# Layer 0 of a two-way scan stack: the gate product written into the sigmoid's SBUF buffer instead of its PSUM bank

## The chip, the cores and the metric

The kernel runs on one core of a Trainium2 chip. The time is in microseconds of the device for one launch of the whole kernel; lower is better. Its engines work at the same time, each through its own queue of instructions in a fixed order: TensorE (PE in the profile) multiplies matrices and writes to PSUM, VectorE (DVE), ScalarE (ACT) and GpSimd (POOL) compute on SBUF and PSUM, and SyncE (SP) issues the transfers. An engine stops at an instruction that waits for a semaphore, and everything behind it in its queue stops too.

## What is computed

Eight batches of 512 tokens with 512 features. A stack of four layers runs over the tokens, once forwards and once backwards, with the same weights for both directions; a fusion product and a feed-forward part follow.

```python
def _mingru(x, Wz, bz, Wh, bh):
    z = jax.nn.sigmoid(jnp.einsum('bsi,hi->bsh', x, Wz) + bz)
    h_tilde = jnp.tanh(jnp.einsum('bsi,hi->bsh', x, Wh) + bh)
    a = jnp.clip(1.0 - z, CLAMP_LO, CLAMP_HI)
    return _linear_scan(a, z * h_tilde)      # h[t] = a[t] * h[t-1] + z[t] * h_tilde[t]
...
    for i in range(L):                        # L = 4
        h_new = _mingru(h, Wz[i], bz[i], Wh[i], bh[i])
        if i > 0:
            h_new = h_new + h
        h = _layernorm(h_new, gamma, beta)
...
h_fwd = _stack(x, ctx_1024, cond_1024, ctx_1024, cond_1024, ...)
h_bwd = _stack(jnp.flip(x, axis=1), ctx_1024, cond_1024, ctx_1024, cond_1024, ...)
x = x + fusion(concatenate([h_fwd, flip(h_bwd)]))
x = x + ffn(layernorm(x))
```

Wz and Wh are the same matrix, and so are the biases, so one matrix product serves sigmoid and tanh. In layer 0 both directions have the same input: the product and its gates are computed once, and two scans, one over the tokens forwards and one backwards, read them.

## The kernel before

The features lie on the 128 partitions in four blocks m = 0 to 3, the 512 tokens along the free axis. A **job** is (batch, direction, layer); the 56 jobs stand in the list `JOBS` in an order written out by hand, and a layer-0 job serves both directions, so there are eight of them, at places 0, 1, 12, 17, 26, 31, 40 and 45 of the list. Each job has four gate products, numbered i = 4k + m through the whole program. They go through these steps:

- `mm` (TensorE, L498): twelve matmuls of 128x512 into the PSUM bank `GATE[i % 3]`, one of three banks that the gates take in turn. Before it overwrites the bank it waits until the scan of product i - 3 is done (`s_sc`).
- `gates` (ScalarE, L794 and L795): the sigmoid of minus the product, which is 1 - z, goes to the SBUF buffer `yb[i % 3]`, and the tanh goes back into the PSUM bank.
- `keep` (GpSimd, L1519): the clipped copy `ab[i % 3]` of `yb`, which is the reference's a.
- `blend` (VectorE, L1070): (1 - yb) times the tanh, written over the tanh in the PSUM bank.
- `scan` (VectorE): from layer 1 on, one scan (L1082) of `ab` and the bank, written over `yb`, and GpSimd adds the layer's input (`add`, L1528). In layer 0 there are two scans: L1090 forwards into `H[s]`, L1091 backwards into `H[s + 1]`.

After that a job's output is normalized over the features: `tokens` (TensorE, L518) turns it with 128x128 transposes into five PSUM banks used as a ring, `stats` (VectorE, L1102 and L1105) takes mean and variance into `mvp`, `inv` (GpSimd, L1537 to L1547) makes scale and shift by four small instructions on 128x2 values (`vep`, `nmp`, `rsp`, `nbp`), `norm` (ScalarE, L806) writes `ntok`, `back` (TensorE, L532) turns it back, `feature` (ScalarE, L831 and L835) and `low` (VectorE, L1114) split it into a high part `AH` and a rest `AL`, from which the next layer's products are made.

What sets the order is the queue of each engine, written out in slots: one slot per job, in which every engine does a fixed mixture of steps of that job and of its neighbours. In VectorE's slot the job's four scans stand among the `low` and `stats` steps of other jobs. GpSimd has, beside `keep`, `add` and `inv`, the preparation of weights: rests of the layer weights at the start (`low_weights`, L1560 and L1562), and from the middle on the pieces of the later weights (`excess`, L1601 and L1603, and `rest`, L1611). After the last job comes the second part of the kernel (fusion, L552; feed-forward, L583 and L602), which the change leaves alone; its instructions L1221, L1281 and L1295 on VectorE and L1648 on GpSimd are quoted below.

Of the kernel before, what the change touches and what calls it, by code (L numbers as in the profile page):

```python
# [7 lines left out]
ALU = mybir.AluOpType  # L8
# [21 lines left out]
def behind(j):  # L30
# [12 lines left out]
JOBS = [  # L43
# [23 lines left out]
def place(t):  # L67

    return 2 * (t[0] % 2) + t[1]
# [144 lines left out]
def pixart_block(nc, x, wt, cond, fwt, fb, gamma, beta, fct, lnw, lnb, pjt, out):  # L214
# [8 lines left out]
    def sb(stack, name, shape, dt=F32):  # L223
        return stack.enter_context(nc.sbuf_tensor(name, shape, dt))

    def sem(name):
        return ctx.enter_context(nc.semaphore(name))
# [50 lines left out]
    for s in (0, 1, 3, 2):  # L278
        AH[s] = sb(p1, f"AH{s}", [128, KC, S], F32R)
        AL[s] = sb(p1, f"AL{s}", [128, KC, S], F32R)  # L280
    H = [sb(p1, f"H{s}", [128, KC, S]) for s in range(4)]
# [3 lines left out]
    yb = [sb(p1, f"yb{i}", [128, S]) for i in range(3)]  # L285
    ab = [sb(p1, f"ab{i}", [128, S]) for i in range(3)]
# [54 lines left out]
    GATE = PS[0:3]  # L341
# [29 lines left out]
    s_wd, s_nc, s_cn, s_a, s_sf, s_sc, s_bs, s_ag, s_ve, s_nm = (  # L371
        sem(n) for n in ("s_wd", "s_nc", "s_cn", "s_a", "s_sf", "s_sc", "s_bs", "s_ag", "s_ve", "s_nm"))
# [8 lines left out]
    s_c, s_wp, s_p, s_v, s_rs, s_nb, s_xr, s_xb, s_pp, s_pl = (  # L381
        sem(n) for n in ("s_c", "s_wp", "s_p", "s_v", "s_rs", "s_nb", "s_xr", "s_xb", "s_pp", "s_pl"))
# [25 lines left out]
    def stored(t):  # L408

        return 16 * (t[0] // 2 + 1)  # L410

    @block.tensor
    def _(e):
# [62 lines left out]
        def mm(k, m):  # L476

            if k is None:
                return
            b, d, l = JOBS[k]  # L480
            s, i = place(JOBS[k]), 4 * k + m
            if i >= 3:
                e.wait_ge(s_sc, i - 2)
            n = 0
            for q in range(KC):
                if m == 0:
                    e.wait_ge(s_al, LOWS[("x", b, q) if l == 0 else ("h", TAIL[(b, d, l - 1)], q)])
                    if k == JOB[(0, 0, l)]:
                        if l == 0:
                            e.wait_ge(s_w0, q + 1)  # L490
                        else:
                            e.wait_ge(s_wh, 4 * l - 3 + q)
                        if (l, q) in WEIGHT_P:
                            e.wait_ge(s_wp, WEIGHT_P.index((l, q)) + 1)
                        else:
                            e.wait_ge(s_wd, WEIGHT_D.index((l, q)) + 1)
                for w, a in ((WH[l], AH[s]), (WL[l], AH[s]), (WH[l], AL[s])):
                    r = e.matmul(GATE[i % 3][:], w[:, q, m * 128:(m + 1) * 128], a[:, q, :], start=(n == 0), stop=(n == 11))  # L498
                    n += 1
            r.then_inc(s_mm, 1)  # L500
# [142 lines left out]
        back("x", 0, 0)  # L643
        fold_row(1)
        mm(0, 0)
        mm(0, 1)
        back("x", 1, 0)
        back("x", 1, 2)
        mm(0, 2)
        back("x", 1, 3)  # L650
        back("x", 1, 1)
# [96 lines left out]
        for j in range(NB * NC):  # L748
            b, c = j // NC, j % NC
# [313 lines left out]
    def _(e):  # L1063
        def blend(k, m):
            if k is None:
                return
            i = 4 * k + m
            c = i % 3
            e.wait_ge(s_t, i + 1)
            e.scalar_tensor_tensor(GATE[c][:], yb[c][:], 1.0, GATE[c][:], ALU.subtract, ALU.mult, reverse0=True).then_inc(s_p, 1)  # L1070

        def scan(k, m):
            if k is None:
                return
            b, d, l = JOBS[k]
            i = 4 * k + m
            c = i % 3
            e.wait_ge(s_a, i + 1)
            e.wait_ge(s_p, i + 1)
            if l > 0:  # L1080
                rv = slice(None, None, -1) if d else slice(None)
                e.tensor_tensor_scan(yb[c][:, rv], ab[c][:, rv], GATE[c][:, rv], 0.0, ALU.mult, ALU.add).then_inc(s_sc, 1)  # L1082
                return
            s = 2 * (b % 2)
            if b >= 2 and m == 0:
                e.wait_ge(d_hs[s], stored((b - 2, 0, 3)))
                e.wait_ge(d_hs[s + 1], stored((b - 2, 1, 3)))

                e.wait_ge(s_t1, max(T1N[("T", TAIL[(b - 2, i, 3)], p, 1)] for i in (0, 1) for p in (0, 1)) + 1)
            e.tensor_tensor_scan(H[s][:, m, :], ab[c][:], GATE[c][:], 0.0, ALU.mult, ALU.add).then_inc(s_sf, 1)  # L1090
            e.tensor_tensor_scan(H[s + 1][:, m, :][:, ::-1], ab[c][:, ::-1], GATE[c][:, ::-1], 0.0, ALU.mult,  # L1091
                                 ALU.add).then_inc(s_sc, 1)

        def stats(tau, pr):
# [252 lines left out]
        low("x", 0, 3)  # L1347
        low_weights(1, 0)
        blend(0, 0)
        scan(0, 0)  # L1350
        blend(0, 1)
        low("x", 1, 0)
        scan(0, 1)
        blend(0, 2)
        low("x", 1, 1)
        low("x", 1, 2)
        scan(0, 2)
        blend(0, 3)
        low("x", 1, 3)
# [111 lines left out]
        for j in range(NB * NC):  # L1471
            b, c = j // NC, j % NC
# [510 lines left out]
```

## Time and profile before

| | us |
|---|---|
| median of 3 runs | 1561.7 (1561.46 to 1562.28) |
| the profiled execution's own time | 1561.99 |
| its span in the profile | 1559.8 |
| TensorE busy | 1526.0 (98%) |
| VectorE busy | 1343.0 (86%) |
| ScalarE busy | 1027.5 (66%) |
| GpSimd busy | 1033.5 (66%) |

The profile is of one execution. Busy time is the sum of the time in which an engine has an instruction under way; matmuls overlap, so a group's mean duration (408 ns for a 128x512 matmul) is longer than the distance at which they follow each other. The granted clock of TensorE is 1.0 of its full speed, so it runs at the higher of its two levels, 2.4 GHz, throughout. The layers take the first 890 us, in which VectorE is busy to nine tenths and more in most slices.

### The profile page before, as it was taken

The numbers are of one execution on the slowest core, as the hardware profiler recorded it, in microseconds if no ns is written. First come the engines' busy times: TensorE is split into PE (matmuls) and PEld (weight loads), VectorE is DVE, ScalarE is ACT, GpSimd is POOL, SyncE is SP. The second block draws the span as 40 slices with busy tenths as digits, with TensorE's granted clock in tenths as the row PEclk, the third lists the DMA queues.
The fourth block names the chain that finished last, engine by engine and source line by source line (L and its number), as shares of the span: only waits on it lengthen the run. The fifth ranks groups of instructions, "written<-read, shape, count | busy, mean of one in ns | idle before, by whom it ended". The sixth has DMA issues, their size and how long they took to land.

```text
span 1559.8 us, 22974 instructions
## 1 busy us (share of the span) xinstructions
PE 1526.0 (98%) x7690; PEld 1256.8 (81%) x7690; DVE 1343.0 (86%) x1919; ACT 1027.5 (66%) x1689; POOL 1033.5 (66%) x1267
## 2 busy tenths in 40 slices
PE   6999999999999999999999999999999999999999
PEld 4777888788878788888888878888888888888887
DVE  7997989989999989899888878798888878787876
ACT  6888979889687898687897544544444444444454
POOL 4766766767868678777688745465556556565566
PEclk9999999999999999999999999999999999999999
DMA  4111121413312111212124462020202021111101
GB/s 169 38 65 55 70 101 34 162 41 108 109 41 84 39 55 68 95 55 83 67 82 163 156 217 61 1 88 21 89 21 88 21 69 40 62 48 32 36 14 41
DMA packets 72865, 112.66 MB, mean 72 GB/s; under 512 B 5159, under 2 KB 37927, under 8 KB 69678
## 3 DMA queue, kind: packets, MB, share of 16 engines
q1 hardware_dynamic: 72750, 111.21, 21.1%
q8 instruction: 62, 1.02, 0.3%
q14 instruction: 53, 0.43, 0.1%
HBM read 73.43 MB, written 37.76 MB: 71 GB/s over the span
## 4 chain that ended last, share of the span: by engine, by line
PE 70%; DVE 5%; ACT 4%; issue 1%; POOL 1%; POOLq 0%; ACTq 0%; DVEq 0%
PE ps L498 21%; PE ps L583 15%; PE ps L602 15%; PE ps L552 11%; PE ps L518 3%; PE ps L532 3%; DVE bnp L1102 1%; ACT H L831 1%; ACT AH L835 1%; PE ps L565 1%; DVE H L1091 1%; DVE H L1090 1%; DVE AL L1114 1%; ACT ps L795 1%; ACT yb L794 1%
## 5 line engine op out<-in xcount | busy, mean ns | idle before, releaser
L498 PE MATMUL ps<-AH,WH 128*128 128x512 f32 x896 | 366.0, 408 | 8.9 <-DVE H L1091 6.8
L498 PE MATMUL ps<-AL,WH 128*128 128x512 f32 x896 | 350.6, 391 | 0.0
L498 PE MATMUL ps<-AH,WL 128*128 128x512 f32 x896 | 349.7, 390 | 0.0
L1648 POOL TENSOR_TENSOR acq<-acq,sq 128x512 f32<-128x512 f32 x120 | 181.8, 1515 | 151.6 <-ACT sq L926 151.1
L1528 POOL TENSOR_TENSOR H<-H,yb 128x512 f32<-128x512 f32 x192 | 250.6, 1306 | 34.6 <-DVE yb L1082 28.2
L1082 DVE TENSOR_TENSOR_SCAN yb<-ab,ps 128x512 f32<-128x512 f32 x192 | 232.4, 1211 | 10.7 <-POOL ab L1519 3.1
L913 ACT ACTIVATE g<-ps 128x512 f32<-128x512 f32 x128 | 76.4, 597 | 249.6 <-PE ps L583 249.6
L794 ACT ACTIVATE yb<-ps,ncnd 128x512 f32<-128x512 f32 x224 | 157.7, 704 | 121.7 <-PE ps L498 118.6
L1519 POOL TENSOR_SCALAR ab<-yb 128x512 f32<-128x512 f32 x224 | 139.0, 621 | 118.5 <-ACT yb L794 106.4
L1281 DVE SCALAR_TENSOR_TENSOR gl<-g,wcol,gh 128x512 fp32r<-128x512 f32 x118 | 133.9, 1135 | 93.3 <-ACT gh L923 93.3
L498 PEld LDWEIGHTS ps<-AH,WH 128*128 128x128 f32 x896 | 168.6, 188 | 46.0 <-DVE H L1091 9.3
L498 PEld LDWEIGHTS ps<-AL,WH 128*128 128x128 f32 x896 | 168.2, 188 | 36.4
L498 PEld LDWEIGHTS ps<-AH,WL 128*128 128x128 f32 x896 | 169.0, 189 | 29.0
L1102 DVE BATCH_NORM_STATS2 bnp<-ps 128x6 f32<-128x512 f32 x256 | 165.2, 685 | 30.6 <-PE ps L518 29.7
L1295 DVE TENSOR_TENSOR acc<-acc,g 128x512 f32<-128x512 f32 x120 | 189.2, 1577 | 0.0
L1070 DVE SCALAR_TENSOR_TENSOR ps<-yb,ps 128x512 f32<-128x512 f32 x224 | 152.3, 680 | 21.7 <-ACT ps L795 20.9
L1114 DVE TENSOR_TENSOR AL<-ps,AH 128x512 fp32r<-128x512 f32 x224 | 147.0, 674 | 19.9 <-ACT AH L835 19.1
L831 ACT ACTIVATE H<-ps,bet,gam 128x512 f32<-128x512 f32 x192 | 155.1, 808 | 3.1 <-PE ps L532 2.9
L806 ACT ACTIVATE ntok<-ps,nbp,rsp 128x512 f32<-128x512 f32 x192 | 139.3, 782 | 16.4 <-POOL nbp L1547 15.8
L835 ACT ACTIVATE AH<-ps 128x512 fp32r<-128x512 f32 x224 | 139.6, 628 | 3.3 <-PE ps L532 3.3
L518 PE MATMUL ps<-ident,H 128*128 128x128 f32 x1024 | 132.6, 273 | 7.4 <-ACT ntok L806 6.4
L518 PEld LDWEIGHTS ps<-ident,H 128*128 128x128 f32 x1024 | 117.5, 140 | 24.7 <-ACT ntok L806 8.6
(172 smaller groups left out, 3308.6 us busy)
## 6 DMA issues: line engine op xcount, KB each, us to landing
hs_scratch<-H SPq DMA_DIRECT2D x16, 1024.0 KB, 5.6
hc<-hs_scratch SPq DMA_DIRECT2D x32, 512.0 KB, 4.4
xr<-in_x SPq DMA_DIRECT2D x32, 256.0 KB, 4.5
out<-ob SPq DMA_DIRECT2D x32, 256.0 KB, 2.2
xbuf<-in_x SPq DMA_DIRECT2D x7, 1024.0 KB, 7.9
RAW<-in_wt SPq DMA_DIRECT2D x16, 256.0 KB, 6.6
stg<-in_fct SPq DMA_DIRECT2D x16, 256.0 KB, 3.1
stg<-in_pjt SPq DMA_DIRECT2D x16, 256.0 KB, 3.2
```

The costliest lines, as they stand in the source:

```text
L498: r = e.matmul(GATE[i % 3][:], w[:, q, m * 128:(m + 1) * 128], a[:, q, :], start=(n == 0), stop=(n == 11))
L518: r = e.transpose(RING[n % 5][:, m * 128:(m + 1) * 128], H[s][:, m, c:c + 128], ident[:])
L552: r = e.matmul(FUSED[u, h][:], a[u % 2][:, q, :], w[:, q, :], start=(n == 0), stop=(n == 11))
L583: r = e.matmul(HIDDEN[j % 2][:], FC[q][:, c * 128:(c + 1) * 128], a[b % 2][:, q, :], start=(n == 0), stop=(n == 7))
L602: r = e.matmul(PROJ[t][:], a[BUFFER[j]][:, t * 128:(t + 1) * 128], PJ[c], start=(c == 0 and a is gh), stop=(c == NC - 1 and a is gl))
L794: e.activation(yb[c][:], GATE[c][:], ACT.Sigmoid, bias=ncnd[:, l, m:m + 1], scale=-1.0).then_inc(s_y, 1)
L831: e.activation(H[s][:, m, :], RING[n][:], ACT.Identity, bias=bet[:, m:m + 1], scale=gam[:, m:m + 1]).then_inc(s_h, 1)
L1082: e.tensor_tensor_scan(yb[c][:, rv], ab[c][:, rv], GATE[c][:, rv], 0.0, ALU.mult, ALU.add).then_inc(s_sc, 1)
L1102: e.bn_stats(bnp[:, r, i, :], RING[BANK[u] % 5][:]).then_inc(s_bs, 1)
L1295: e.tensor_tensor(acc[b % 2][:], acc[b % 2][:], g[j % 2][:], ALU.add).then_inc(f_s1, 1)
L1528: e.tensor_tensor(H[s][:, m, :], H[s][:, m, :], yb[i % 3][:], ALU.add).then_inc(s_v, 1)
L1648: e.tensor_tensor(acq[b % 2][:], acq[b % 2][:], sq[:], ALU.add).then_inc(f_s2, 1)
```

## The change

In layer 0 the blend writes its product into `yb[i % 3]`, over the sigmoid, and both scans read it there, so that the PSUM bank is free after the blend. The product i of `mm` therefore waits for the blend of i - 3 (`s_p`) where i - 3 is of layer 0, and for its scan as before in the other layers. Since the blend now overwrites what `keep` reads, it waits for GpSimd's `keep` of the same product (`s_a`), for which before only the scan waited. The sigmoid of product i still waits for the scans of i - 3 before it writes `yb`.

```diff
@@ mm
-            if i >= 3:
+            if i >= 3 and JOBS[(i - 3) // 4][2] == 0:
+                e.wait_ge(s_p, i - 2)
+            elif i >= 3:
                 e.wait_ge(s_sc, i - 2)
@@ blend
             e.wait_ge(s_t, i + 1)
-            e.scalar_tensor_tensor(GATE[c][:], yb[c][:], 1.0, GATE[c][:], ALU.subtract, ALU.mult, reverse0=True).then_inc(s_p, 1)
+            if JOBS[k][2] == 0:
+                e.wait_ge(s_a, i + 1)
+            dst = yb[c] if JOBS[k][2] == 0 else GATE[c]
+            e.scalar_tensor_tensor(dst[:], yb[c][:], 1.0, GATE[c][:], ALU.subtract, ALU.mult, reverse0=True).then_inc(s_p, 1)
@@ scan
-            e.tensor_tensor_scan(H[s][:, m, :], ab[c][:], GATE[c][:], 0.0, ALU.mult, ALU.add).then_inc(s_sf, 1)
-            e.tensor_tensor_scan(H[s + 1][:, m, :][:, ::-1], ab[c][:, ::-1], GATE[c][:, ::-1], 0.0, ALU.mult,
+            e.tensor_tensor_scan(H[s][:, m, :], ab[c][:], yb[c][:], 0.0, ALU.mult, ALU.add).then_inc(s_sf, 1)
+            e.tensor_tensor_scan(H[s + 1][:, m, :][:, ::-1], ab[c][:, ::-1], yb[c][:, ::-1], 0.0, ALU.mult,
                                  ALU.add).then_inc(s_sc, 1)
```

No instruction is added, removed or moved on any engine: 32 blends write elsewhere, 64 scans read their second input elsewhere, and the waits of the products behind 32 of them and of the 32 blends differ.

## Rows read from the trace of the kernel before

**Rows 1.** the page: the span line and the engines' busy times.

```profile
span 1559.8 us, 22974 instructions
...
PE 1526.0 (98%) x7690; PEld 1256.8 (81%) x7690; DVE 1343.0 (86%) x1919; ACT 1027.5 (66%) x1689; POOL 1033.5 (66%) x1267
```

**Rows 2.** whom TensorE waited for: us in total, times, longest.

```profile
PE ps L498 <- DVE H L1091: 6.8, 6, 1.9
PE ps L518 <- ACT ntok L806: 6.4, 9, 0.7
```

**Rows 3.** three lines' instructions: duration in ns min/median/max, first and last start.

```profile
L1091 DVE TENSOR_TENSOR_SCAN H<-ab,ps x32: 1191/1194/1197, 25.6 to 742.3; 128x512 f32<-128x512 f32 x32
...
L1295 DVE TENSOR_TENSOR acc<-acc,g x120: 677/1779/1791, 922.5 to 1546.6; 128x512 f32<-128x512 f32 x120
...
L1537 POOL TENSOR_SCALAR vep<-mvp x128: 191/191/1663, 39.1 to 917.1; 128x2 f32<-128x2 f32 x128
```

**Rows 4.** timeline of VectorE, then GpSimd: start us, length us, line.

```profile
1013.17 1.78 DVE L1295 TENSOR_TENSOR acc<-acc,g 128x512 f32<-128x512 f32 x1
...
917.55 1.20 DVE L1221 TENSOR_TENSOR hcl<-hc,hch 128x1024 fp32r<-128x1024 f32 x1
...
1013.06 1.33 POOL L1648 TENSOR_TENSOR acq<-acq,sq 128x512 f32<-128x512 f32 x1 [5.50 <-ACT sq L926]
...
917.15 1.66 POOL L1537 TENSOR_SCALAR vep<-mvp 128x2 f32<-128x2 f32 x1 [1.71 <-DVE mvp L1105]
```

**Rows 5.** timeline of VectorE, batch 4's layer-0 job.

```profile
435.49 0.68 DVE L1070 SCALAR_TENSOR_TENSOR ps<-yb,ps 128x512 f32<-128x512 f32 x1
436.36 1.22 DVE L1090 TENSOR_TENSOR_SCAN H<-ab,ps 128x512 f32<-128x512 f32 x1 [0.19 <-POOL ab L1519]
...
438.61 0.67 DVE L1070 SCALAR_TENSOR_TENSOR ps<-yb,ps 128x512 f32<-128x512 f32 x1
...
439.99 1.21 DVE L1090 TENSOR_TENSOR_SCAN H<-ab,ps 128x512 f32<-128x512 f32 x1
...
447.20 0.30 DVE L1105 BATCH_NORM_AGGREGATE mvp<-bnp 128x2 f32<-128x6 f32 x2
```

**Rows 6.** timeline of GpSimd over the same stretch.

```profile
435.71 0.62 POOL L1519 TENSOR_SCALAR ab<-yb 128x512 f32<-128x512 f32 x1
436.41 1.28 POOL L1528 TENSOR_TENSOR H<-H,yb 128x512 f32<-128x512 f32 x1
437.77 0.61 POOL L1519 TENSOR_SCALAR ab<-yb 128x512 f32<-128x512 f32 x1
438.48 0.77 POOL L1601 TENSOR_SCALAR stg<-raw,th,nth 128x512 f32<-128x512 f32 x1
439.33 1.29 POOL L1603 TENSOR_TENSOR stg<-raw,stg 128x512 f32<-128x512 f32 x1
...
448.85 0.19 POOL L1547 TENSOR_TENSOR nbp<-nmp,rsp 128x2 f32<-128x2 f32 x1
```

**Rows 7.** timeline of ScalarE and TensorE there; idle time and releaser in brackets.

```profile
450.01 1.45 ACT L806 ACTIVATE ntok<-ps,nbp,rsp 128x512 f32<-128x512 f32 x2
...
449.78 0.50 PE L498 MATMUL ps<-AH,WH 128*128 128x512 f32 x1 [0.97 <-DVE H L1091]
...
452.64 1.91 PE L532 MATMUL ps<-ident,ntok 128*128 128x128 f32 x16
```

**Rows 8.** timeline at the start: VectorE, GpSimd, TensorE.

```profile
24.47 1.22 DVE L1090 TENSOR_TENSOR_SCAN H<-ab,ps 128x512 f32<-128x512 f32 x1
...
26.71 0.67 DVE L1070 SCALAR_TENSOR_TENSOR ps<-yb,ps 128x512 f32<-128x512 f32 x1
...
23.89 1.57 POOL L1560 TENSOR_SCALAR RAW<-RAW,gam 128x512 f32<-128x512 f32 x1
25.54 1.30 POOL L1562 TENSOR_TENSOR WL<-RAW,WH 128x512 fp32r<-128x512 f32 x1
...
35.47 0.50 PE L498 MATMUL ps<-AH,WH 128*128 128x512 f32 x1 [1.12 <-DVE AL L1114]
```

## The prediction

> **What bounds the kernel now.** I read the page first, to see which engine could set the end: TensorE is busy for 1526.0 of a span of 1559.8 us, VectorE for 1343.0 [rows 1]. All that TensorE does not do costs time, and at most some 34 us can be won. The second view is the table of waits, to see what TensorE's gaps come from [rows 2]. Six times a product waited for a layer-0 backward scan (L1091), 6.8 us in sum: once for each of the six layer-0 jobs after the start, and this is what the edit to `mm` removes. Nine times a transpose of `tokens` waited for ScalarE's `norm`, 6.4 us in sum, with nothing over 0.7 us; that chain comes from VectorE's `stats` through GpSimd's `inv`. So TensorE is held up a little, by a VectorE that is behind for a moment after a layer-0 job. The third view is the timeline around such a job, to see whether VectorE has room there [rows 5 to 7]; in it VectorE has almost no idle time, so a delay on it is handed on.
>
> **The wait that goes.** In batch 4 the product at 449.78 sat idle for 0.97 us for the scan [rows 7]. The blend of that product, third of the job, had ended more than 3 us before that, so by the new rule TensorE would go on at once. The gain is bounded by nothing and by the 6.8 us of the table. I don't expect to keep it even if nothing else changed: the next waits of TensorE, for ScalarE's `norm` [rows 2], hang on VectorE's queue, which this wait does not speed up, so they grow by most of what is won here.
>
> **The wait that comes.** The blend must now wait for `keep`. For block 0 of batch 4 the blend began at 435.49, while `keep` began at 435.71 and took 0.62 [rows 5, 6]: it would start at 436.35, 0.86 later. The forward scan had stood 0.19 idle for the same `keep` and began at 436.36; behind a blend of 0.68 it now begins at 437.1, 0.7 later. For the other blocks `keep` is done before the blend (437.77 plus 0.61 against 438.61) as long as GpSimd is not late. Queued behind the waiting blend on VectorE are the scans, the `low` and `stats` steps of other jobs, and TensorE and ScalarE wait for those.
>
> **The scans' second input, the largest term.** A scan now reads two SBUF tensors, which none in this trace does. What the trace shows is how the two classes of VectorE instruction behave beside GpSimd. With one input in PSUM, the 32 backward scans take 1191 to 1197 ns whatever GpSimd is doing [rows 3], and the scan at 436.36 ran its 1.22 us under a GpSimd add begun at 436.41 [rows 5, 6]. With two inputs in SBUF, the additions of L1295 take 677 ns at best, but 1779 in the median and 1791 at most [rows 3]: the one at 1013.17 took 1.78 us, and GpSimd's two-input add had begun at 1013.06 for 1.33 us; VectorE stood until it had ended [rows 4]. It goes the other way too: GpSimd's small `vep` takes 191 ns, but 1663 at most [rows 3], and that one, at 917.15, ended at 918.81, with the two-input subtraction of VectorE that ran from 917.55 to 918.75 [rows 4]. So the two exclude each other for whole instructions, and take turns. The price of a scan in SBUF is thus bounded by nothing, as for the scans now, and by the remainder of a GpSimd instruction each, up to 1.3 us; I take the second, because the rows nearest to it in what they read (two SBUF tensors, same size) have it.
>
> The Trainium skill says the same for the class: on its page "SBUF — State Buffer", under "Who interferes with whom", a VectorE instruction with two SBUF inputs contends with a GpSimd instruction that reads SBUF, and one with at most one SBUF input does not. That is a rule that speaks against this change; rows 3 and 4 agree with it for additions and subtractions, and no run here shows a scan of this kind.
>
> **Batch 4 worked out.** Two scans take 2.25 us on VectorE (436.36 to 438.61), 1.12 each [rows 5]. Forward scan of block 0: ready at 437.1, held by the add begun at 436.41 (1.28 us) until 437.6, done at 438.7. `keep` of block 1, which was to start at 437.77, gets its turn next, to 439.3 [rows 6]. Backward scan: 439.3 to 440.4. The blend of block 1 starts at 440.4 where it was 438.61: VectorE is 1.8 late. GpSimd resumes at 440.4 with L1601 (0.77) and L1603 (1.29) [rows 6], to 442.5; the forward scan of block 1, at 439.99 before, is ready at 441.8 and held for 0.6; a `keep` slips in before the backward one, 0.5. VectorE is 2.9 late when it comes to the aggregate of 447.20, which starts `inv` [rows 5]. Right behind it stand the scans of block 2 and 3, and the four small instructions of `inv` fall between them: the first waits for a forward scan (1.1), the second for the backward one (1.1), the last for the next forward scan (0.9 of it), so `inv` takes 3.0 longer. `nbp`, before from 448.85 to 449.04 [rows 6], ends 5.9 later. ScalarE's two norms started at 450.01, 0.97 after it, and took 1.45, to 451.46; TensorE's transposes started at 452.64, 1.18 after that [rows 7]. That is all the cover there is: 2.15. TensorE is 5.9 - 2.15 = 3.8 late there. If the small instructions are not held, it is 2.9 - 2.15 = 0.8 at this place, but some 3 at the next `norm` for which TensorE already waits today, as VectorE is itself about 3.2 late by the end of the four scan pairs and has no idle time in which to catch up before. I take 3.2 for a job, with 1.8 and 3.8 as the bounds. The absent wait of 0.97 is in this, as all is reckoned against the starts of before.
>
> Batches 4 to 7 have this pattern: 4 x 3.2 = 12.8. Batches 2 and 3 come before L1601 and L1603 begin, and keep only the 1.8 of block 0 and the 3.0 of `inv`, less the same cover of 2.15: 2.65 each, which I round to 2.6, so 5.2.
>
> **The start.** Beside the first products GpSimd prepares weights with L1560 (1.57 us) and L1562 (1.30), one after the other [rows 8]. The scan at 24.47 would be held until 25.46, 1.0, and its backward partner by L1562, 1.2: 2.2 for the product. The pair stands beside the second product too, 2.2. The third has its blend behind a late `keep`, 0.7. In sum 5.1 on a VectorE that goes from 24.47 to the end of the fourth product's `low` without a pause, and there TensorE already waits 1.12 us for it, at 35.47 [rows 8], so all 5.1 reach TensorE. Batch 1 meets the same two instructions twice more, but TensorE has work of its own there; between 0 and 4, I take 1.0.
>
> **The sum.** 5.1 + 1.0 + 5.2 + 12.8 = 24.1 us. On the profiled execution's 1561.99 that is 1586.1, and as the median lay 0.3 lower, **1585.8 us**, 1.5% slower. Nothing after the last job changes.
>
> **The rivals.**
> 1. *The scans don't exclude GpSimd.* A scan takes 1.12 us for 512 columns, nearly twice an addition, and may read so slowly that both are served. Then the new `keep` wait remains, about 1.2 at the start, where GpSimd's `keep` stands behind the long preparations, and 0.7 of VectorE in five jobs, which eats the removed stall at the next `norm`: between 0 and +2 in all, 1562.5. For it: no scan in the trace reads two SBUF tensors. Against it: all other two-input instructions are held.
> 2. *Faster: the freed bank carries through.* The same, but `norm` comes earlier too, since ScalarE's queue starts earlier when the product does. All of L1091's 6.8 us would be kept [rows 2]: 1561.7 - 6.8 = 1554.9. It decides if ScalarE's lateness and not VectorE's aggregate sets `norm`. Against it: a saturated VectorE, and the `keep` wait.
> 3. *Excluded, but small instructions are not*, and part of the delay falls into gaps: 1.8 for four jobs, 1.0 for two, 3 at the start, so 12: 1574. I count it in the forecast's own range.
>
> That the change doesn't do what it says is possible only in part: where VectorE is late, the blend is late too, and a product may wait for it in place of the scan. This is inside the first case.
>
> **How the numbers follow.** The exclusion, with its range of 1571 (rival 3 and a little less) to 1597 (3.8 for four jobs, 2.6 for two, 9 at the start, and some 5 for delays that feed one another), has 0.76; rival 1 has 0.17, rival 2 0.07. A tenth of the first case lies outside its range. To leave out no more than 2 in 10 the whole range must reach down to rival 1: 1561 to 1597. A measurement of this kernel can tell 0.2%, 3 us, from no change. Slower by more than that: 0.76 and 0.03 of rival 1, 0.79; within: 0.13, nearly all of rival 1 with a little of rival 2; faster: 0.08, rival 2 and a tail of rival 1.
>
> **What the new profile would show.** If right: the scans of layer 0 no longer take some 1.2 us each but reach 2 us and more, GpSimd's `vep`, `nmp` or `nbp` show durations over 1 us around 232 to 745 us, the blend has idle time put down to GpSimd's `ab`, no product waits for L1091's successor, and TensorE's waits for `norm` or for `low` at the start are longer by some 20 us in sum. If the scans keep their 1.2 us, the largest term is wrong and rival 1 or 2 holds. If they are held but TensorE's waits grow by less than 10 us, it is the cover that I have misjudged.

## The result, and the profile after

| | before, us | changed, us |
|---|---|---|
| median | 1561.85 (1561.46 to 1562.28, 4 runs) | 1586.11 (1585.08 to 1587.89, 4 runs) |
| ratio | | 1.0154 (95% interval 1.0141 to 1.0167) |
| span of the profiled execution | 1559.8 | 1584.6 |
| GpSimd busy | 1033.5 | 1073.5 |

The change costs 24.3 us, 1.5%. The page of the changed kernel, its lines that answer to [rows 1], and the costliest new idle time:

```profile
span 1584.6 us, 23006 instructions
...
PE 1534.8 (97%) x7690; PEld 1260.9 (80%) x7690; DVE 1354.9 (86%) x1919; ACT 1028.8 (65%) x1689; POOL 1073.5 (68%) x1267
...
L534 PE MATMUL ps<-ident,ntok 128*128 128x128 f32 x896 | 118.2, 281 | 29.7 <-ACT ntok L808 16.7
```

The page counts 32 instructions more: the blends' waits for `s_a`, the same 32 as in the run with the blend's wait alone (23006) and absent where only the scans' input is changed (22974). TensorE and VectorE are hardly busier (8.8 and 11.9 us more), GpSimd by 40 us, though its compute instructions are the same 1267: time in which an instruction of it is held counts as busy. The line of `back` (L534, before L532) now has 29.7 us of idle time before it. The table of waits of TensorE, which answers to [rows 2] (us in sum, times, longest):

```profile
PE ps L534 <- ACT ntok L808: 16.7, 10, 2.6
...
PE ps L500 <- DVE AL L1119: 7.4, 7, 2.4
PE ps L520 <- ACT ntok L808: 6.9, 9, 1.2
```

The six waits for L1091 are gone, as the diff says. In their place stand ten waits of `back` for ScalarE's `norm`, 16.7 us (0.7 before), and seven of products for VectorE's `low` (7.4, before 1.1 in one).

**The held instructions.** Durations of the layer-0 scans and of three of the small instructions of `inv`, in ns min/median/max, which answer to [rows 3]:

```profile
L1095 DVE TENSOR_TENSOR_SCAN H<-ab,yb x32: 1201/1225/1929, 23.8 to 765.8; 128x512 f32<-128x512 f32 x32
...
L1096 DVE TENSOR_TENSOR_SCAN H<-ab,yb x32: 1192/1200/2256, 25.0 to 767.0; 128x512 f32<-128x512 f32 x32
...
L1542 POOL TENSOR_SCALAR vep<-mvp x128: 192/193/1664, 42.4 to 941.9; 128x2 f32<-128x2 f32 x128
...
L1544 POOL TENSOR_SCALAR nmp<-mvp x96: 192/193/1103, 42.6 to 885.8; 128x2 f32<-128x2 f32 x96
...
L1552 POOL TENSOR_TENSOR nbp<-nmp,rsp x96: 195/197/1098, 43.7 to 886.8; 128x2 f32<-128x2 f32 x96
```

The backward scans took at most 1197 ns before; now the slowest takes 2256. The small instructions that take 0.19 us alone show up to 1.1 us (`vep` had its one of 1.66 already before). Most scans are still at 1.2: only those that met a reading GpSimd are longer. (In this kernel no instruction of GpSimd has a PSUM bank as an operand; all read and write SBUF.)

**Batch 4's job.** VectorE and GpSimd in the timeline of the changed kernel, which answer to [rows 5, 6]. TensorE's work was 12.05 us later than before when the job began, so a start at 448.53 stands against 435.49 + 12.05 = 447.54.

```profile
448.53 0.69 DVE L1075 SCALAR_TENSOR_TENSOR yb<-yb,ps 128x512 f32<-128x512 f32 x1 [0.91 <-POOL ab L1524]
449.31 1.56 DVE L1095 TENSOR_TENSOR_SCAN H<-ab,yb 128x512 f32<-128x512 f32 x1
450.79 1.56 DVE L1096 TENSOR_TENSOR_SCAN H<-ab,yb 128x512 f32<-128x512 f32 x1
452.28 0.66 DVE L1075 SCALAR_TENSOR_TENSOR yb<-yb,ps 128x512 f32<-128x512 f32 x1
...
453.46 1.93 DVE L1095 TENSOR_TENSOR_SCAN H<-ab,yb 128x512 f32<-128x512 f32 x1
455.31 1.19 DVE L1096 TENSOR_TENSOR_SCAN H<-ab,yb 128x512 f32<-128x512 f32 x1
...
461.39 0.30 DVE L1110 BATCH_NORM_AGGREGATE mvp<-bnp 128x2 f32<-128x6 f32 x2
461.61 1.20 DVE L1095 TENSOR_TENSOR_SCAN H<-ab,yb 128x512 f32<-128x512 f32 x1
462.73 1.20 DVE L1096 TENSOR_TENSOR_SCAN H<-ab,yb 128x512 f32<-128x512 f32 x1
```

```profile
447.81 0.61 POOL L1524 TENSOR_SCALAR ab<-yb 128x512 f32<-128x512 f32 x1
448.51 1.28 POOL L1533 TENSOR_TENSOR H<-H,yb 128x512 f32<-128x512 f32 x1
449.88 1.40 POOL L1524 TENSOR_SCALAR ab<-yb 128x512 f32<-128x512 f32 x1
451.38 1.55 POOL L1606 TENSOR_SCALAR stg<-raw,th,nth 128x512 f32<-128x512 f32 x1
453.02 1.28 POOL L1608 TENSOR_TENSOR stg<-raw,stg 128x512 f32<-128x512 f32 x1
...
461.77 1.02 POOL L1542 TENSOR_SCALAR vep<-mvp 128x2 f32<-128x2 f32 x1 [0.42 <-DVE mvp L1110]
462.88 1.04 POOL L1544 TENSOR_SCALAR nmp<-mvp 128x2 f32<-128x2 f32 x1
463.88 0.71 POOL L1549 TENSOR_TENSOR rsp<-vep,nhalf 128x2 f32<-128x2 f32 x1
464.73 1.09 POOL L1552 TENSOR_TENSOR nbp<-nmp,rsp 128x2 f32<-128x2 f32 x1
```

The blend waits 0.91 us for `keep`. The forward scan of block 0 is held by the add begun at 448.51, which has 0.48 us to go, and takes 1.56. Then `keep` of block 1, which was issued at 449.88, gets its turn and the backward scan waits for it, 1.56. L1606 in turn waits for that scan (1.55 instead of 0.77), and L1608 holds the next forward scan, 1.93. The aggregate of 461.39 is 2.1 us late against 447.20 + 12.05. Then `vep`, `nmp` and `nbp` each wait for one scan: 1.02, 1.04 and 1.09 us instead of 0.19 or 0.20. ScalarE and TensorE behind it, as in [rows 7]:

```profile
465.85 1.45 ACT L808 ACTIVATE ntok<-ps,nbp,rsp 128x512 f32<-128x512 f32 x2 [2.50 <-POOL nbp L1552]
...
459.73 0.50 PE L500 MATMUL ps<-AH,WH 128*128 128x512 f32 x1 [0.64 <-DVE AL L1119]
...
467.35 1.96 PE L534 MATMUL ps<-ident,ntok 128*128 128x128 f32 x16 [2.56 <-ACT ntok L808]
```

`norm` starts at 465.85, after 2.50 us of idle time, and the transposes of `back`, 452.64 + 12.05 = 464.69 by the old offset, at 467.35, after 2.56 us.

**Where the 24 us arise.** How much later than before ScalarE takes up the first product of a job (start of its sigmoid, from the timelines of both kernels). A row's gain is what the layer-0 job between them cost:

| through the job of | lateness in, us | lateness out, us | cost, us | forecast, us |
|---|---|---|---|---|
| batches 0 and 1 | -0.85 | 7.8 | 8.6 | 6.1 |
| batch 2 | 7.8 | 11.1 | 3.3 | 2.6 |
| batch 3 | 11.1 | 12.05 | 0.9 | 2.6 |
| batch 4 | 12.05 | 14.8 | 2.75 | 3.2 |
| batch 5 | 14.8 | 19.2 | 4.4 | 3.2 |
| batch 6 | 19.2 | 22.2 | 3.0 | 3.2 |
| batch 7 | 22.2 | 24.7 | 2.5 | 3.2 |

Between these jobs the lateness doesn't move by more than 0.1 us, and it is still 24.7 at the last job (the start of a run varies by about a microsecond, -0.85 here, so the costs add up to 25.5). The 3.3 and the 4.4 of batches 2 and 5, and the 8.6 of the start, hold something that the others don't: TensorE's granted clock falls for a moment there, about 1.7 us each time (last section).

### The profile page after: what moved, and what is told of

Its sections match the earlier page's. It is cut to its first block, busy times and chain, and to the rows that moved or that the text cites. A ratio compares the mean times of both kernels' runs of the same rounds, so it can differ in the third digit from the quotient of the medians.

```text
span 1584.6 us, 23006 instructions
## 1 busy us (share of the span) xinstructions
PE 1534.8 (97%) x7690; PEld 1260.9 (80%) x7690; DVE 1354.9 (86%) x1919; ACT 1028.8 (65%) x1689; POOL 1073.5 (68%) x1267
## 3 DMA queue, kind: packets, MB, share of 16 engines
q8 instruction: 62, 1.02, 0.3%
## 4 chain that ended last, share of the span: by engine, by line
PE 60%; POOL 8%; DVE 6%; ACT 4%; issue 3%; POOLq 0%; DVEq 0%; ACTq 0%
PE ps L585 15%; PE ps L604 14%; PE ps L500 14%; PE ps L554 11%; POOL H L1533 2%; PE ps L534 2%; PE ps L520 2%; POOL ab L1524 1%; DVE bnp L1107 1%; DVE H L1095 1%; PE ps L567 1%; ACT H L833 1%; ACT ntok L808 1%; ACT AH L837 1%; DVE AL L1119 1%
## 5 line engine op out<-in xcount | busy, mean ns | idle before, releaser
L1087 DVE TENSOR_TENSOR_SCAN yb<-ab,ps 128x512 f32<-128x512 f32 x192 | 232.4, 1211 | 10.4 <-POOL ab L1524 3.1
L1524 POOL TENSOR_SCALAR ab<-yb 128x512 f32<-128x512 f32 x224 | 155.4, 694 | 91.9 <-ACT yb L796 78.6
L1119 DVE TENSOR_TENSOR AL<-ps,AH 128x512 fp32r<-128x512 f32 x224 | 147.2, 675 | 22.2 <-ACT AH L837 21.9
L534 PE MATMUL ps<-ident,ntok 128*128 128x128 f32 x896 | 118.2, 281 | 29.7 <-ACT ntok L808 16.7
L1075 DVE SCALAR_TENSOR_TENSOR ps<-yb,ps 128x512 f32<-128x512 f32 x192 | 130.7, 681 | 18.5 <-ACT ps L797 17.8
L534 PEld LDWEIGHTS ps<-ident,ntok 128*128 128x128 f32 x896 | 102.8, 144 | 49.5 <-ACT ntok L808 29.4
```

Source lines behind the costliest of these rows:

```text
L534: r = e.transpose(RING[n % 5][:, i * 128:(i + 1) * 128], ntok[w][:, i, m * 128:(m + 1) * 128], ident[:])
L1524: e.tensor_scalar(ab[c][:], yb[c][:], 1.0 - 1e-8, 1e-8, ALU.min, ALU.max).then_inc(s_a, 1)
```

## The experiments

Theory 1 says that a scan with two SBUF inputs and a reading GpSimd instruction exclude each other. Theory 2 says that the new wait of the blend is what costs. The first two runs do one part each.

**The SBUF input alone.** On the kernel before:

```diff
-            e.tensor_tensor_scan(H[s][:, m, :], ab[c][:], GATE[c][:], 0.0, ALU.mult, ALU.add).then_inc(s_sf, 1)
-            e.tensor_tensor_scan(H[s + 1][:, m, :][:, ::-1], ab[c][:, ::-1], GATE[c][:, ::-1], 0.0, ALU.mult,
+            e.tensor_tensor_scan(H[s][:, m, :], ab[c][:], yb[c][:], 0.0, ALU.mult, ALU.add).then_inc(s_sf, 1)
+            e.tensor_tensor_scan(H[s + 1][:, m, :][:, ::-1], ab[c][:, ::-1], yb[c][:, ::-1], 0.0, ALU.mult,
```

> The kernel before, with one thing changed: the layer-0 scans take the sigmoid's SBUF buffer as their second input, while the gate product still goes to PSUM (so layer 0's values are other ones). No new wait for keep, and the products still wait for the scans. Theory 1, scans with two SBUF inputs and GpSimd exclude each other: nearly all of the 24.3 us of the change, 1581 to 1588 us. Theory 2, the blend's new wait for keep is the cause: 1562 us. Theory 3, the exclusion costs only together with the wait: 1570 to 1575 us.

Measured: 1584.74 us (1584.06 to 1585.75), ratio 1.0143 (1.0128 to 1.0158), against 1562.53 for the kernel before on the same chip: 22.2 us. Its backward scans, and the wait that the change removes:

```profile
L1091 DVE TENSOR_TENSOR_SCAN H<-ab,yb x32: 1186/1201/2309, 24.9 to 763.3; 128x512 f32<-128x512 f32 x32
...
PE ps L498 <- DVE H L1091: 12.1, 7, 1.9
```

No semaphore was touched, and the scans reach 2309 ns. Theory 3 falls, and theory 2 as the main cause. Before, the wait for L1091 was 6.8 us in six times; late scans make it 12.1.

**The blend's wait alone.** On the kernel before:

```diff
             e.wait_ge(s_t, i + 1)
+            if JOBS[k][2] == 0:
+                e.wait_ge(s_a, i + 1)
```

> The kernel before, with the layer-0 blends waiting for keep and nothing else. Theory 1: VectorE is 0.6 to 0.9 us later in five of the later jobs and about 1.2 at the start, of which most is covered or reaches TensorE once: 1562 to 1566 us. Theory 2: 1580 us or more.

Measured: 1567.17 us (1565.55 to 1567.79), ratio 1.0031 (1.0019 to 1.0043): 4.6 us over the 1562.53 of the kernel before on the same chip, and above theory 1's 1562 to 1566. The blend of batch 4's block 0, and TensorE's wait for L1091 (here L1093):

```profile
437.16 0.70 DVE L1072 SCALAR_TENSOR_TENSOR ps<-yb,ps 128x512 f32<-128x512 f32 x1 [0.85 <-POOL ab L1521]
...
PE ps L498 <- DVE H L1093: 10.5, 6, 2.0
```

The 0.85 us of the blend are as forecast from [rows 5, 6]. What I had missed is who catches them: as long as the product waits for the scan, the whole delay goes on to it, and the waits of 6.8 become 10.5. By the sigmoids, batches 2 to 6 cost 0.4, 0, 0.65, 0.7 and 0.9 us, and batch 7 costs 2.7 (below, under the clock). The one run of the six whose mean granted clock is 1.000 took 1565.55, within what was expected; the other five, at 0.999, took 1566.67 to 1567.79. So the 1.2 us over the upper bound may be the clock. The costs of the two parts, 22.2 and 4.6, do not add: together they would be more than the whole.

**The early release undone.** The changed kernel, with the products waiting for the scans:

```diff
-            if i >= 3 and JOBS[(i - 3) // 4][2] == 0:
-                e.wait_ge(s_p, i - 2)
-            elif i >= 3:
+            if i >= 3:
                 e.wait_ge(s_sc, i - 2)
```

> The changed kernel, but all products wait for the scans again, as before. Theory 1: the early release wins little, as the waits of TensorE behind a layer-0 job hang on inv and norm: 1586 to 1589 us. If the early release wins what it removed (6.8 us and more with late scans), 1593 us or more.

Measured: 1586.36 us (1585.3 to 1587.5), ratio 1.0153 (1.0136 to 1.0170); the changed kernel itself has 1.0154. The release wins nothing that can be measured; the two intervals leave room for some 3 us either way (estimate). TensorE's waits show why:

```profile
PE ps L498 <- DVE H L1094: 12.8, 7, 2.3
...
PE ps L532 <- ACT ntok L806: 3.2, 6, 1.8
```

Here 12.8 us of waits for the scan stand where the changed kernel has none, and in exchange `back` waits for `norm` for 3.2 us and not for 16.7. TensorE waits once or the other time for the same late queues.

**The start alone.** The change in batches 0 and 1 only (`in_sbuf(i)` stands for layer 0 and the batches and blocks named, in `mm`, `blend` and `scan`):

```diff
+    return l == 0 and (b < 2)
```

> The change in batches 0 and 1 alone. In the trace of the changed kernel the sigmoids are 7.8 us late once both jobs are through; if the delays of the jobs add up, this is 1569.6 us. My prediction had 6.1 for it (1568). If the later jobs alone make the time, 1562.

Measured: 1571.23 us (1569.66 to 1571.91), ratio 1.0055 (1.0040 to 1.0070), 8.7 us. That is more than a third of the loss for a quarter of the scans, and above my 6.1. The clock falls three times in its profiled run (0.67 at 39 to 42 us, 0.52 at 57 to 60, 0.70 at 90 to 93), which is up to 5 us of it (estimate, 1.7 each). VectorE, GpSimd and TensorE at the start of the changed kernel, which answer to [rows 8]:

```profile
23.84 1.23 DVE L1095 TENSOR_TENSOR_SCAN H<-ab,yb 128x512 f32<-128x512 f32 x1
24.98 2.26 DVE L1096 TENSOR_TENSOR_SCAN H<-ab,yb 128x512 f32<-128x512 f32 x1
...
24.70 1.47 POOL L1567 TENSOR_TENSOR WL<-RAW,WH 128x512 fp32r<-128x512 f32 x1
26.25 1.40 POOL L1524 TENSOR_SCALAR ab<-yb 128x512 f32<-128x512 f32 x1
...
38.23 0.50 PE L500 MATMUL ps<-AH,WH 128*128 128x512 f32 x1 [2.38 <-DVE AL L1119]
```

Only one of the two scans of the first product is held, not both: `keep` had been early, L1565 had begun before the forward scan, which still took 1.23, and L1567 then held the backward one. TensorE waits 2.38 us for `low` at 38.23, and 2.04 more in front of that, at 34.20, where before it had not waited.

**Blocks 0 and 1, and blocks 2 and 3, of batches 2 to 7.**

```diff
+    return l == 0 and (b >= 2 and m < 2)
```
```diff
+    return l == 0 and (b >= 2 and m >= 2)
```

> The change in batches 2 to 7 and there for the blocks 0 and 1 alone; all other products as before. In the changed kernel these two blocks made VectorE 2.1 us late in batch 4 (the aggregate that starts inv), without its small instructions being held. Theory 1 with a shared cover of about 2.15 us: the third block's scans are late by that and the product behind them waits for them, 1 to 2 us for each of six jobs, 1568 to 1574 us. If the cover hides it: 1562 to 1564.

> The change in batches 2 to 7 for the blocks 2 and 3 alone, the ones beside inv. Three small instructions of GpSimd are held for about 0.85 us each, 2.5 in sum, of which 2.15 is covered, and the product behind block 2 no longer waits: 0 to 1 us for a job, 1562 to 1568 us. The two halves must then stay well below the whole, which has 15 us in batches 2 to 7, if it is the shared cover that decides; if the delays simply add up, the two halves together give 15 us.

Measured: blocks 0 and 1, 1575.49 us (1574.28 to 1578.81), ratio 1.0092 (1.0075 to 1.0109), 13.0 us; blocks 2 and 3, 1564.85 us (1564.24 to 1566.42), ratio 1.0017 (1.0008 to 1.0027), 2.4 us. The first was above the 6 to 12 us expected, the second as expected. In the profiled run of the first the clock falls twice, once of them at 81 to 87 us, before any changed job. The wait of the product for the scan in the first, and of `back` for `norm` in the second:

```profile
PE ps L506 <- DVE H L1103: 11.4, 6, 1.9
```

```profile
PE ps L540 <- ACT ntok L814: 10.8, 9, 1.9
```

Together the halves give 15.4, and the start 8.7: 24.1 of the 24.3 us. These sums hold different numbers of falls of the clock, so the batches without one are the better test: by the sigmoids the halves cost 2.1 and 0.6 us in batch 4, 2.3 and 0.6 in batch 6, 2.1 and 0.6 in batch 7, and the whole 2.75, 3.0 and 2.5. So the delays add up, and what I had said of a cover that both share is not borne out. With blocks 0 and 1 alone all of VectorE's 2 us arrive at the product behind block 2, as in the run before; there is no cover on that way. With blocks 2 and 3 alone `back` waits up to 1.9 us, but the removed stall pays for part of it. The third block's scans, which stand beside `inv`, are the cheaper half.

**The dose.** The SBUF input in all layers, as in the first run but with L1082 too:

```diff
-                e.tensor_tensor_scan(yb[c][:, rv], ab[c][:, rv], GATE[c][:, rv], 0.0, ALU.mult, ALU.add).then_inc(s_sc, 1)
+                e.tensor_tensor_scan(yb[c][:, rv], ab[c][:, rv], yb[c][:, rv], 0.0, ALU.mult, ALU.add).then_inc(s_sc, 1)
```

> The dose: as in the run with the SBUF input alone, but in all four layers: 256 scans instead of 64 take the sigmoid's SBUF buffer as second input (values are other ones, the products go to PSUM, no wait is changed). Theory 1: 22 us for 64 scans; the 192 others stand beside a GpSimd that is as busy, so 60 to 110 us more, 1645 to 1700 us, and the scans at L1082 take up to 2.4 us instead of 1.2. If the cost were tied to layer 0 alone (two scans in a row, the bank that is freed): 1585 to 1590 us.

Measured: 1671.23 us (2 runs, 1670.81 and 1671.65), ratio 1.0698 (1.0677 to 1.0719), 108.8 us: 86.6 more than the 64 scans of layer 0, 0.45 us for each further scan against 0.35. About a fifth of the 108.8 us and a third of the 22.2 is the clock (mean 0.987 of 1669.7 us and 0.995 of 1582.5; an estimate, as if all of it were lost). The cost is in the operands, not in layer 0. In this kernel VectorE's group of L1082 with its idle time, TensorE's wait for `norm`, and GpSimd's `keep`:

```profile
L1082 DVE TENSOR_TENSOR_SCAN yb<-ab,yb 128x512 f32<-128x512 f32 x192 | 252.3, 1315 | 79.9 <-POOL ab L1519 75.1 <-issue 0.4
...
PE ps L532 <- ACT ntok L806: 42.5, 34, 3.0
...
L1519 POOL TENSOR_SCALAR ab<-yb x224: 614/617/1598, 22.5 to 999.0; 128x512 f32<-128x512 f32 x112
```

The scans of L1082 are longer by only 0.1 us in the mean (1211 before, and up to 2322 ns as expected); the larger part lies in the 75.1 us in which VectorE sat idle for `keep`, which is itself held, up to 1598 ns. Which side pays depends on who comes second.

**A narrower neighbour.** The changed kernel, with GpSimd's L1601 and L1603 on one column in the slots of batches 4 to 7's layer-0 jobs:

```diff
+            c = slice(0, 1) if narrow else slice(0, 512)
-            e.tensor_scalar(stg2[n % 2][:], raw[n % 2][:], th[:, w:w + 1], nth[:, w:w + 1], ALU.min, ALU.max).then_inc(s_pp, 1)
+            e.tensor_scalar(stg2[n % 2][:, c], raw[n % 2][:, c], th[:, w:w + 1], nth[:, w:w + 1], ALU.min, ALU.max).then_inc(s_pp, 1)
...
-            e.tensor_tensor(stg2[n % 2][:], raw[n % 2][:], stg2[n % 2][:], ALU.subtract).then_inc(s_pl, 1)
+            e.tensor_tensor(stg2[n % 2][:, c], raw[n % 2][:, c], stg2[n % 2][:, c], ALU.subtract).then_inc(s_pl, 1)
```

> The changed kernel, in which GpSimd's weight preparation works on one column instead of 512 in the slots of the four layer-0 jobs of batches 4 to 7 (so four pieces of the later weights are wrong). Theory 1: the forward scan of block 1 is held 0.7 us by the wide one, and VectorE's share of a job's delay goes down by 0.7 to 1.2: 3 to 5 us less than the changed kernel, 1581 to 1583 us. If GpSimd's wide instructions don't matter: 1586.

Measured: 1583.17 us (1580.49 to 1585.25), ratio 1.0133 (1.0118 to 1.0148), 2.9 us less than the changed kernel's 1586.11, at the low edge of the 3 to 5 expected; the intervals of the two ratios overlap (the changed kernel's is 1.0141 to 1.0167), so this difference alone would not decide. The forward scan of block 1 and GpSimd's L1601 (here L1607) beside it:

```profile
452.01 1.21 DVE L1095 TENSOR_TENSOR_SCAN H<-ab,yb 128x512 f32<-128x512 f32 x1
...
449.94 1.12 POOL L1607 TENSOR_SCALAR stg<-raw,th,nth 128x1 f32<-128x1 f32 x1
```

What decides is the trace. The scan is back at 1.21 us from 1.93, and batches 4, 6 and 7 cost 2.05, 2.2 and 1.8 us in place of 2.75, 3.0 and 2.5, 0.7 to 0.8 less each. Batch 5 costs 2.05 in place of 4.4, but there the clock does not fall in this run. Batches 2 and 3, which the narrowing leaves alone, cost 3.35 and 0.9 as before it. The one-column instruction still takes 1.12 us, since it is held as long as a wide one: width matters when GpSimd holds, not when it is held.

## Why the prediction was right

The forecast was 1585.8 and the time is 1586.11. The mechanism was right and is shown; the closeness is luck, because a cost that the prediction has no term for, TensorE's clock, filled what its terms had too much. Step by step:

- **The wait that goes.** Right: all six are gone, and undoing the release changes the time by nothing measurable.
- **The scans' second input.** Right, and shown: it alone gives 22.2 of the 24.3 us, without a semaphore moved. Taking the upper of the two bounds, from the additions of [rows 3, 4], was the decision on which the forecast stood, and a scan behaves as they do. One of its rows shows less than was read from it: the `vep` of 917.15 began 0.40 us before the subtraction, while VectorE was in another instruction, a copy out of PSUM (L1307, from 916.98 for 0.65 us); only the rest of its 1.66 us lies beside the subtraction.
- **The wait that comes.** The 0.86 us were right (0.91 in the changed kernel, 0.85 alone), but rival 1, which rested on it, was sized too small: 0 to +2 where it measures 4.6 (about 4 between runs at a mean clock of 1.000, 1565.55 against 1561.33 to 1561.65).
- **Batch 4.** The order of who holds whom is as worked out up to the backward scan of block 1, into which I had let a `keep` slip; none was due, since the next `keep` waited for its sigmoid. VectorE was 1.6 late at the blend of block 1 (1.8 forecast) and 2.1 at the aggregate (2.9). `inv` took 2.6 longer (3.0). `norm` was 3.8 late (4.9 by the forecast's own sum) and `back` 2.66 (3.8); the job cost 2.75, for which I had taken 3.2.
- **All six later jobs.** The same reading for each, from the timelines of both kernels, in us later than before and against the offset at the job's begin. Cost is the column of the table above.

| batch | VectorE at the aggregate | `inv` longer by | `back` later by | cost |
|---|---|---|---|---|
| 2 | 1.1 | 2.6 | 1.6 | 3.3 |
| 3 | 0.9 | 2.0 | 0.8 | 0.9 |
| 4 | 2.1 | 2.6 | 2.7 | 2.75 |
| 5 | 2.2 | 2.6 | 2.7 | 4.4 |
| 6 | 2.3 | 2.6 | 2.8 | 3.0 |
| 7 | 2.2 | 1.9 | 2.0 | 2.5 |
| forecast, 2 and 3 | 1.8 | 3.0 | 2.6 | 2.6 |
| forecast, 4 to 7 | 2.9 | 3.0 | 3.8 | 3.2 |

The cover between `nbp` and `back` is 2.1 us in every row, as forecast (2.15), and the sum of the first two columns less this cover gives the third. Both held terms were too large throughout. The cost goes beyond the lateness of `back` by 1.7 us in batches 2 and 5, and those are the two jobs behind which the clock fell.
- **Batch 3** was the cheapest, 0.9 and not 2.6. VectorE was only 0.9 late at the aggregate, and in `inv` the last small instruction was hardly held, because VectorE does another instruction first there (L1210, 0.74 us, in front of the forward scan of block 3):

```profile
324.67 0.49 POOL L1552 TENSOR_TENSOR nbp<-nmp,rsp 128x2 f32<-128x2 f32 x1
```

That the removed stall was largest there (1.92 us, [rows 2]) is not the cause: without the release batch 3 costs 0.96 as well. It costs 2.5 with the SBUF input alone and 1.6 with blocks 2 and 3 alone, but in those two runs the clock falls right behind its wait (0.67 at 321 to 324 us, 0.51 at 315 to 318), and not in the changed kernel (0.9), without the release (0.96) or with blocks 0 and 1 alone (0.6).
- **The start.** 6.1 forecast, and 8.6 by the lateness (8.7 alone). The first job cost less than its 5.1: the lateness goes from -0.85 to 2.76 us at the first product of batch 1, since only one scan of each pair was held (1.07 and 1.06 us more). Batch 1, for which I had taken 1.0, cost 5.0, to 7.74. The term that failed is the step from "TensorE has work of its own there" to a small cost: `back` waited 1.83 us at 56.65, and TensorE's clock fell twice there, at 39 to 45 and at 54 to 60 us (below), which is up to 3.4 of the 5.0 (estimate, 1.7 each).
- **The sum.** So the total was closer than its terms: the start and batches 2 and 5 were 2.5, 0.7 and 1.2 too low, batches 3, 4 and 7 were 1.7, 0.5 and 0.7 too high. The four falls of the clock in the profiled run make up to 6.8 us (estimate), for which the sum has nothing; the terms that it does have, 24.1, would have come out at 17.5 to 18.7. The mechanism was right; the agreement within a microsecond is luck.

On the pages, the rule of the Trainium skill (page "SBUF — State Buffer", "Who interferes with whom") that two SBUF inputs contend with GpSimd's reads holds here for a scan too: the backward ones take 1192 to 2256 ns with two, 1191 to 1197 with one in PSUM. The rows of batch 4 above also show the two taking turns: a waiting GpSimd instruction gets in between two scans that are issued back to back.

## What to carry to other kernels

Before an operand of VectorE is moved from PSUM to SBUF, count the SBUF inputs: with the second one the instruction shares GpSimd's fate, and here both engines waited out what was left of each other's instruction, with one kind of exception (last section). The victims that are easiest to overlook are GpSimd's tiny instructions on a dependency chain, which are held as long as big ones. And a buffer freed earlier wins nothing if what waits next hangs on the same late queue.

## What I had not expected

**The clock of TensorE.** Batches 4 and 5 have the same program around their layer-0 job and the same wait of `back` (2.56 and 2.58 us), but cost 2.75 and 4.4 us. After the wait of batch 4 the granted clock stayed at 1.0; after that of batch 5 it fell to 0.64 of full speed in the mean of the next 3 us, that is, for a part of them to the lower of the two levels, 1.2 GHz. Stretches of the changed kernel with their granted clock (column PEclk), and the transposes in the second:

```profile
core 0: us, PE busy (x) PEld busy (x) DVE busy (x) ACT busy (x) POOL busy (x), PEclk, DMA share, GB/s
...
468.00:471.00 3.00, 3.00 (x21) 2.66 (x19) 2.81 (x4) 3.00 (x6) 2.63 (x3) 1.00 0.01 3
...
547.00:550.00 3.00, 3.00 (x18) 2.90 (x18) 2.71 (x4) 3.00 (x6) 2.22 (x3) 0.64 0.00 0
550.00:553.00 3.00, 3.00 (x12) 2.32 (x12) 2.10 (x3) 2.54 (x5) 2.92 (x3) 0.79 0.03 12
...
546.80 2.70 PE L534 MATMUL ps<-ident,ntok 128*128 128x128 f32 x16 [2.58 <-ACT ntok L808]
```

They took 2.70 us, against 1.96 for the same sixteen at 467.35. Batch 2 shows it as well (3.3 us; 0.58 and 0.85 in the 6 us from 247), and so does the start, twice: after the waits at 34.20 and 38.23 the clock is 0.72 from 39 to 45 us, and after the wait of 1.83 at 56.65 it is 0.54 from 57 to 60, where it was 1.0 before. The mean over the span is 0.996. With the blend's wait alone it happened once, in batch 7: 2.7 us and not 0.65, after a wait of 2.05 us at 744.61. The profiled run of the kernel before shows 1.0 throughout the layers. Of its 22 runs beside the experiments, the 8 listed with a mean clock of 1.000 took 1561.33 to 1562.07 us, the 14 with 0.999 took 1561.62 to 1563.26; so it seems to happen to that kernel too, once or so in a run.

Each fall costs TensorE about 1.7 us of full speed (the two rows from 547: 0.36 and 0.21 of 3 us; estimate), and batch 5 costs 1.65 more than batch 4. What decides whether it comes is open, and the length of the last wait alone does not: it followed waits of 1.61 us (the start alone, 91.49), 1.83 (here, 56.65), 1.91 (the SBUF input alone, 321.20) and 1.95 (blocks 2 and 3, 314.31), and did not follow 1.92 (the kernel before, 311.85), 2.35 (the blend's wait alone, 35.78), 2.56 and 2.57 (here, batches 4 and 6). No run was made to take it away. It may also be why the runs of one changed kernel spread more (1580.5 to 1585.3 with the narrow neighbour, at mean clocks of 0.997 and 0.994) than those of the kernel before.

**Small instructions pay in full.** `vep`, `nmp` and `nbp` on two columns lost 0.83 to 0.91 us each to scans of 1.2. I had counted on it from a single row of before; it is now seen in full in the jobs of batches 2, 4, 5 and 6, and in part in 3 (`nbp` lost 0.30) and 7 (`nmp` and `rsp`, about 0.9 each).

**How long a scan is held.** It is the same for `keep`, which reads one tensor, as for the additions, which read two: what is left of GpSimd's instruction, less 0.12 to 0.14 us. `keep`, begun at 449.88 for 1.40 us, had 0.49 left when the backward scan of 450.79 came, and the scan took 0.35 more than its 1.21; the add of 448.51 had 0.48 left at 449.31, and the scan took 0.35 more; L1608 had 0.84 left at 453.46, for 0.72; L1567 1.19 at 24.98, for 1.05. The exception is L1565, a one-input instruction of 1.57 us. Begun at 23.04, it held the forward scan of 23.84 not at all (1.23 us), though 0.77 was left, nor that of 28.96. But it does hold one that comes early:

```profile
63.25 1.81 POOL L1565 TENSOR_SCALAR RAW<-RAW,gam 128x512 f32<-128x512 f32 x1 [1.34 <-PE ps L456]
63.61 1.65 DVE L1096 TENSOR_TENSOR_SCAN H<-ab,yb 128x512 f32<-128x512 f32 x1
```

Its 1.81 us are its own 1.57 behind the 0.24 for which the scan before held it, so it ran from 63.49; the scan of 63.61 was held for 0.44, to 64.05, while L1565 went on to 65.06. So it stood in the scan's way for its first 0.56 us and not for the last 1.0. It is why only one scan of each pair was held at the start, where the forecast had two. Why this instruction differs from `keep` no run here tells.
